# Sums by source: deeper rings, and SyncE reads its start places four at a time without a range check

## The chip, the cores and the metric

One core of one Trainium2 chip runs the whole program. The metric is the device time of one execution, in microseconds (us); lower is better.

## The reference

A graph of 6250 nodes (256 features each) and 100000 edges (sorted by target `dst`) goes through four graph layers. What matters here is what layers 0 and 1 sum over the edges of one node:

```python
h = relu(layernorm(x))
support = h @ weight                                  # layer 0
msgs = support[src_or_dst] * edge_weight[:, None]
out = segment_sum(msgs, ..., num_segments=6250)       # summed by the edge's source
edge_proj = edge_attr @ W_sum + b_sum                 # layer 1
sum3d = segment_sum(edge_proj, src, num_segments=n)   # by source too
out_deg = segment_sum(ones, src, num_segments=n)
```

In layer 0 the call passes `src` as the row to sum into and `dst` as the row to read. So for each source node three things are summed over its edges: the weighted rows h[dst] (256 numbers), the edge attributes (128 numbers), and a count (1). The products with the weights come after the sums. Layers 2 (attention by target) and 3 (a gated update with relation vectors) follow; the change does not touch them.

## The kernel before, in words

The program is a chain of stages with a barrier between them: `prepare` (ranks the edges by source and scatters one record per edge into DRAM), `source_sums`, `layers_0_and_1`, `attention`, `layer_2`, `relations_and_layer_3`. Five engines run their own instruction streams and meet at semaphores.

`source_sums` (L721 to L841) is the stage that the change touches. `src_records` holds the edges' records in order of source: 128 attributes, a one, the source, the target, the weight (132 floats, `REC`). Nodes lie in 49 blocks of 128. A tile is 128 consecutive records that belong to one block; there are `TILES` = 832 of them, whatever the graph, so the last ones of the list are empty: their start place is clamped to EDGES, where 128 padding records lie, all of them with target 0. About 100000/128 + 49/2, some 806 tiles, hold edges. One tile passes through these steps:

- SyncE (L755 to L761) has the tile's start place in a register and issues the load of its 128 records into `s_rec[k]`. Before it reuses a slot it waits until the tile that had the slot is summed (L760). A turn is `UNROLL` = 8 tiles. At its head (L756) SyncE reads eight start places into registers, and for each a range check runs: one FUSED_REGOPS and one SEQ_ASSERT.
- ScalarE (L773, L774) turns the target into an integer index and the source into a place within the block.
- GpSimd (L781, L782) waits for that index and issues an indirect DMA that gathers 128 rows of h, 1 KB each, into `s_row[k]`.
- VectorE (L811, L813) makes two one-hot matrices of 128x128, `s_hot` and the weighted `s_hotw`.
- TensorE (L790 to L795) waits for both one-hots, for the gathered rows, and for the PSUM bank (four of them) to be free, then does two matmuls into one bank: weighted rows, and attributes with the count.
- VectorE (L820) adds the bank to the block's sums in `nodes`. It does so `LAG` = 4 tiles behind the one-hots, so in its stream add(t-4) stands behind hots(t). At a turn's head (L826) it reads the blocks of eight tiles into registers.

GpSimd has no wait of its own for a free row slot; that order comes from the index, which waits for the record, which waits for the tile `R` = 8 before to be summed. So SyncE's wait at L760 bounds how far the whole chain runs ahead: eight tiles. Every loop runs over turns of R tiles, and the loop's body is unrolled R times on each engine.

Of the kernel before, what the change touches and what calls it, by code (L numbers as in the profile page):

```python
# [21 lines left out]
SP_E, PE_E, DVE_E, ACT_E = (mybir.EngineType.SP, mybir.EngineType.PE, mybir.EngineType.DVE,  # L22
                             mybir.EngineType.Activation)

P = 128
NODES, D = 6250, 256
EDGES, ED = 100000, 128
# [5 lines left out]
UNROLL = 8  # L33
# [3 lines left out]
TILES = -(-(-(-EDGES // P) + BLOCKS) // (2 * UNROLL)) * 2 * UNROLL  # L37
TURNS = TILES // UNROLL
# [6 lines left out]
ONE, SRC, DST, WGT = ED, ED + 1, ED + 2, ED + 3  # L45
NW = D + ED + 1
# [2 lines left out]
ROUNDS = [len(range(k, BLOCKS, TURN_BLOCKS)) for k in range(TURN_BLOCKS)]  # L49
RELS = 16  # L50
ORDER_RANGE = "the order holds each block, 0 to BLOCKS - 1, once"
BLOCK_RANGE = "a tile's block is a count of blocks (1 to BLOCKS) less one, whatever the graph"
DEG_MAX = 511
EPS = 1e-5
# [666 lines left out]
def source_sums(env):  # L721

    nc, c, sb, ps, sem = (env[k] for k in ("nc", "c", "sb", "ps", "sem"))
    acc = env["nodes"]
    R = UNROLL
    LAG = 4
    with nc.cleanup_on_exit(), ExitStack() as ctx:
        rec = sb(ctx, "s_rec", [P, R, REC])
        row = sb(ctx, "s_row", [P, R, D])
        idx = sb(ctx, "s_idx", [P, R], I32)  # L730
        loc = sb(ctx, "s_loc", [P, R])
        hot = sb(ctx, "s_hot", [P, R, P])
        hotw = sb(ctx, "s_hotw", [P, R, P])
        blk = sb(ctx, "s_blk", [1, TILES], I32)
        start = sb(ctx, "s_start", [1, TILES], I32)
        blk_all = sb(ctx, "s_blk_all", [P, TILES], I32)
        nbase = sb(ctx, "s_nbase", [P, TILES])
        sums = [ps(ctx, f"s_sums{k}", [P, 512]) for k in range(4)]

        tables, cleared = sem("s_tables"), sem("s_cleared")  # L740
        rec_in = [sem(f"s_rec_in{k}") for k in range(R)]
        row_in = [sem(f"s_row_in{k}") for k in range(R)]
        idx_ready, loc_ready, hot_ready = sem("s_idx_ready"), sem("s_loc_ready"), sem("s_hot_ready")
        summed, added = sem("s_summed"), sem("s_added")

        with nc.Block() as block:
            @block.sync
            def _(sp):
                sp.dma_start(blk[:], env["table_rows"]["sb"][0:TILES, :].rearrange("t o -> o t")).then_inc(tables, 16)
                sp.dma_start(start[:], env["table_rows"]["ss"][0:TILES, :].rearrange("t o -> o t")).then_inc(tables, 16)  # L750
                sp.dma_start(blk_all[:], env["table_rows"]["sb"][0:TILES, :].rearrange("t o -> o t")
                             .broadcast_to([P, TILES])).then_inc(tables, 16)
                sp.wait_ge(tables, 48)

                def turn(g, opening):  # L755
                    _, firsts = nc.values_load_multi_w_load_instructions(  # L756
                        start[0:1, bass.ds(g * R, R)], engines=(SP_E,), min_val=0, max_val=EDGES)
                    for k in range(R):
                        if not opening:
                            sp.wait_ge(summed, g * R + (k - R + 1))  # L760
                        sp.dma_start(rec[:, k, :], env["src_records"][bass.ds(firsts[k], P), :]).then_inc(rec_in[k], 16)  # L761

                turn(0, True)
                with sp.Fori(1, TURNS) as g:
                    turn(g, False)

            @block.scalar
            def _(ac):
                ac.wait_ge(cleared, 2)
                with ac.Fori(0, TURNS) as g:  # L770
                    for k in range(R):
                        ac.wait_ge(rec_in[k], g * 16 + 16)
                        nc.scalar.activation(idx[:, k:k + 1], rec[:, k, DST:DST + 1], ACT.Copy).then_inc(idx_ready, 1)  # L773
                        nc.scalar.activation(loc[:, k:k + 1], rec[:, k, SRC:SRC + 1], ACT.Identity,  # L774
                                             bias=nbase[:, bass.ds(g * R + k, 1)]).then_inc(loc_ready, 1)

            @block.gpsimd
            def _(gp):
                with gp.Fori(0, TURNS) as g:
                    for k in range(R):  # L780
                        own_wait(gp, idx_ready, g * R + k + 1)  # L781
                        gp.indirect_dma_start(out=row[:, k, :], out_offset=None, in_=env["h0_rows"],  # L782
                                              in_offset=bass.IndirectOffsetOnAxis(ap=idx[:, k:k + 1], axis=0)
                                              ).then_inc(row_in[k], 16)

            @block.tensor
            def _(pe):
                def turn(g, opening):
                    for k in range(R):
                        pe.wait_ge(hot_ready, g * (2 * R) + 2 * k + 2)  # L790
                        pe.wait_ge(row_in[k], g * 16 + 16)
                        if not opening or k >= 4:
                            pe.wait_ge(added, g * R + (k - 4 + 1))
                        nc.tensor.matmul(sums[k % 4][:, 0:D], hotw[:, k, :], row[:, k, :], start=True, stop=True)  # L794
                        nc.tensor.matmul(sums[k % 4][:, D:NW], hot[:, k, :], rec[:, k, 0:ED + 1],  # L795
                                         start=True, stop=True).then_inc(summed, 1)

                turn(0, True)
                with pe.Fori(1, TURNS) as g:
                    turn(g, False)  # L800

            @block.vector
            def _(ve):
                nc.vector.memset(acc[:], 0.0).then_inc(cleared, 1)
                ve.wait_ge(tables, 48)
                nc.vector.tensor_scalar(nbase[:], blk_all[:], -float(P), None, ALU.mult).then_inc(cleared, 1)
                ve.wait_ge(cleared, 2)

                def hots(g, k):
                    ve.wait_ge(loc_ready, g * R + k + 1)  # L810
                    nc.vector.tensor_scalar(hot[:, k, :], c["iota"][:], loc[:, k:k + 1], None,  # L811
                                            ALU.is_equal).then_inc(hot_ready, 1)
                    nc.vector.tensor_scalar(hotw[:, k, :], c["iota"][:], loc[:, k:k + 1], rec[:, k, WGT:WGT + 1],  # L813
                                            ALU.is_equal, ALU.mult).then_inc(hot_ready, 1)

                def add(t, k, b):
                    ve.wait_ge(summed, t + 1)
                    ve.wait_ge(added, t)
                    s = acc[:, bass.ds(b, 1), :]
                    nc.vector.tensor_tensor(s, s, sums[k % 4][:, 0:NW].rearrange("p (a b) -> p a b", a=1),  # L820
                                            ALU.add).then_inc(added, 1)

                def turn(g, opening):
                    lo = 0 if opening else g * R - LAG
                    n = R - LAG if opening else R
                    _, blocks = nc.values_load_multi_w_load_instructions(  # L826
                        blk[0:1, bass.ds(lo, n)], engines=(DVE_E,), min_val=0, max_val=BLOCKS - 1,
                            skip_runtime_bounds_check_because=BLOCK_RANGE)
                    for k in range(R):
                        hots(g, k)  # L830
                        if not opening or k >= LAG:
                            add(g * R + (k - LAG), (k - LAG) % R, blocks[k - LAG if opening else k])

                turn(0, True)
                with ve.Fori(1, TURNS) as g:
                    turn(g, False)
                _, blocks = nc.values_load_multi_w_load_instructions(
                    blk[0:1, TILES - LAG:TILES], engines=(DVE_E,), min_val=0, max_val=BLOCKS - 1,
                            skip_runtime_bounds_check_because=BLOCK_RANGE)
                for k in range(LAG):  # L840
                    add(TILES - LAG + k, R - LAG + k, blocks[k])  # L841
# [962 lines left out]
def relations_and_layer_3(env):  # L1804
# [10 lines left out]
    with nc.cleanup_on_exit(), ExitStack() as ctx:  # L1815
# [35 lines left out]
        def ranked(q, engine):  # L1851

            _, (b,) = nc.values_load_multi_w_load_instructions(
                c["dord"][0:1, bass.ds(q, 1)], engines=(engine,), min_val=0, max_val=BLOCKS - 1,
                skip_runtime_bounds_check_because=ORDER_RANGE)
            return b
# [281 lines left out]
```

## Time and profile before

| what | value |
| --- | --- |
| runs | 5604.88, 5611.56, 5610.76 us; median 5610.76 |
| the profiled execution | 5615.93 us, of which the span (first to last instruction) 5614.1 us |
| `source_sums` | from about 1476 to 2572 us of the span: 1096 us |
| busy there | GpSimd 794.5, VectorE 851.3, TensorE 767.4, ScalarE 330.1 us |
| granted TensorE clock | 0.955 over the span, 0.98 in the stage |

"Busy" counts an engine's work, not its waits and not its sequencer's register and DMA-issuing instructions; SyncE has only such instructions and so no busy time. "Idle before" an instruction is the time in which its engine did nothing, and the arrow names what ended it: another engine's instruction, the landing of a DMA, or "issue", when nothing outside was waited for. The last piece of `source_sums` is the add of tile 831; the barrier and the cleanup behind it take about 2 us, and the next stage's loads follow.

### The profile page before, as it was taken

The page shows a single profiled execution, that of the slowest core. Times are in us where ns is not written, and L with a number is a line of the kernel's source. Part 1 is how long each engine was busy: PE and PEld are TensorE (multiplying, and loading weights), DVE is VectorE, ACT ScalarE, POOL GpSimd, SP SyncE. Part 2 cuts the span into 40 slices and gives each one's busy share as a digit, 9 for nine tenths or more (in the row PEclk, how much of TensorE's full clock was granted, in tenths as well). Part 3 has the DMA queues.
Part 4 walks back from the last instruction along what each step waited for, and adds up shares of the span by engine and source line. Part 5 has one row for each costly group of instructions (what it writes and reads, how often), then busy time and mean ns, then how long its engine had stood idle before and what let it go on. Part 6 is the DMA issues. An engine that isn't in the chain of part 4 may idle for free. (4 is left out here: it accounts for less than half of the span.)

```text
span 5614.1 us, 108115 instructions
## 1 busy us (share of the span) xinstructions
PE 3530.3 (63%) x16558; PEld 2634.7 (47%) x16559; DVE 3950.7 (70%) x14077; ACT 1757.7 (31%) x6303; POOL 3898.1 (69%) x4332
## 2 busy tenths in 40 slices
PE   0000035200277777776768999999989778888887
PEld 0000012100255555554547888888879644554444
DVE  9918999300477777774568888888868766666665
ACT  0000000000133333332337777777756411111111
POOL 2878887776477777775766666666647777676774
PEclk9999999999999999997879999999999889899998
DMA  2232233335355555554323333333322233333332
GB/s 75 76 84 79 76 82 88 87 88 125 76 156 157 157 158 155 157 157 93 94 86 96 94 94 94 95 94 95 94 66 66 88 111 114 103 110 106 108 108 78
DMA packets 491102, 578.41 MB, mean 103 GB/s; under 512 B 114758, under 2 KB 394328, under 8 KB 490945
## 3 DMA queue, kind: packets, MB, share of 16 engines
q0 software_dynamic: 189536, 397.34, 25.4%
q1 hardware_dynamic: 301473, 180.10, 11.8%
q14 instruction: 67, 0.55, 0.0%
q8 instruction: 26, 0.43, 0.0%
HBM read 491.28 MB, written 86.57 MB: 103 GB/s over the span
## 5 line engine op out<-in xcount | busy, mean ns | idle before, releaser
L410 POOL DMA_INDIRECT src_records<-rec,pos_slot x800 | 1005.0, 1256 | 345.2 <-issue 237.0
L1289 POOL DMA_INDIRECT a_row<-h_rows,a_idx x832 | 787.6, 947 | 369.8 <-PE a_p_s L1415 197.1
L1905 POOL DMA_INDIRECT r_row<-h_rows,r_idx x832 | 802.1, 964 | 310.2 <-issue 168.2
L782 POOL DMA_INDIRECT s_row<-h_rows,s_idx x832 | 794.5, 955 | 299.7 <-issue 171.7
L794 PE MATMUL s_sums<-s_row,s_hotw 128*128 128x256 f32 x1664 | 584.9, 434 | 329.8 <-DMA s_row<-h_rows,s_idx 231.7
L1946 PE MATMUL r_p_s<-r_row,r_hot 128*128 128x272 f32 x1664 | 602.2, 474 | 233.2 <-DVE r_row L2080 215.1
L1392 PE MATMUL a_p_q<-nodes,a_hotT 128*128 x1664 | 569.8, 424 | 55.5 <-DVE a_score L1459 54.1
L1946 PEld LDWEIGHTS r_p_s<-r_row,r_hot 128*128 128x128 f32 x1664 | 335.4, 221 | 516.8 <-DVE r_row L2080 233.8
L820 DVE TENSOR_TENSOR nodes<-nodes,s_sums 128x385 f32 x832 | 461.5, 555 | 157.1 <-PE s_sums L795 138.7
L1415 PE MATMUL a_p_s<-a_row,a_masked 128*128 128x257 f32 x1664 | 497.0, 380 | 2.1 <-DVE sums L1496 1.4
L794 PEld LDWEIGHTS s_sums<-s_row,s_hotw 128*128 128x128 f32 x1664 | 253.0, 192 | 477.1 <-issue 369.6
L2088 DVE TENSOR_TENSOR sums<-sums,r_p_s 128x272 f32 x832 | 358.6, 431 | 149.3 <-PE r_p_s L1946 103.2
L773 ACT ACTIVATE s_idx<-s_rec 128x1 int32<-128x1 f32 x832 | 167.9, 202 | 863.3 <-DMA s_rec<-src_records 731.3
L1496 DVE SCALAR_TENSOR_TENSOR sums<-sums,a_fade,a_p_s 128x257 f32 x832 | 399.3, 480 | 41.7 <-PE a_p_s L1415 3.7
L1459 DVE CUSTOM_DVE_ANT_0 a_prod<-a_p_q,a_row 128x258 f32<-128x258 f32 x832 | 353.5, 425 | 104.9 <-ACT a_masked L1338 63.3
L795 PEld LDWEIGHTS s_sums<-s_rec,s_hot 128*128 128x128 f32 x1664 | 323.0, 194 | 46.1
L477 ACT ACTIVATE pos_slot<-pos_src 125x8 int32 x100 | 20.9, 209 | 1014.8 <-DMA rec<-in_edge_attr 991.4
L1415 PEld LDWEIGHTS a_p_s<-a_row,a_masked 128*128 128x128 f32 x1664 | 314.5, 190 | 49.5 <-ACT a_masked L1359 2.3
L795 PE MATMUL s_sums<-s_rec,s_hot 128*128 128x129 f32 x1664 | 326.2, 278 | 0.0
L1338 ACT ACTIVATE a_masked<-a_far,a_score 128x128 f32<-128x128 f32 x832 | 323.7, 389 | 2.0 <-DVE a_score L1459 2.0
L1359 ACT ACTIVATE a_masked<-a_masked,a_mneg 128x128 f32<-128x128 f32 x832 | 324.2, 390 | 0.0
L504 PE MATMUL p_total<-cnt,ones 125*128 125x49 f32 x4 | 1.3, 432 | 492.2 <-DVEq L559 492.2
(308 smaller groups left out, 8747.5 us busy)
## 6 DMA issues: line engine op xcount, KB each, us to landing
s_rec<-src_records SPq DMA_DIRECT2D x832, 66.0 KB
rec<-in_edge_attr SPq DMA_DIRECT2D x100, 500.0 KB
s_row<-h_rows,s_idx POOLq DMA_INDIRECT x832
a_row<-h_rows,a_idx POOLq DMA_INDIRECT x832, 2.8
r_row<-h_rows,r_idx POOLq DMA_INDIRECT x832, 2.8
src_records<-rec,pos_slot POOLq DMA_INDIRECT x800
h_rows<-H SPq DMA_DIRECT2D x1, 6272.0 KB
x_rows<-nodes SPq DMA_DIRECT2D x49, 128.0 KB, 1.9
```

What stands on the lines that cost most here:

```text
L410: gp.indirect_dma_start(out=src_records, out_offset=bass.IndirectOffsetOnAxis(ap=pos_slot[:, k:k + 1], axis=0), in_=rec[:, k, :], in_offse ...
L782: gp.indirect_dma_start(out=row[:, k, :], out_offset=None, in_=env["h0_rows"], in_offset=bass.IndirectOffsetOnAxis(ap=idx[:, k:k + 1], axis=0)
L794: nc.tensor.matmul(sums[k % 4][:, 0:D], hotw[:, k, :], row[:, k, :], start=True, stop=True)
L795: nc.tensor.matmul(sums[k % 4][:, D:NW], hot[:, k, :], rec[:, k, 0:ED + 1], start=True, stop=True).then_inc(summed, 1)
L820: nc.vector.tensor_tensor(s, s, sums[k % 4][:, 0:NW].rearrange("p (a b) -> p a b", a=1), ALU.add).then_inc(added, 1)
L1289: gp.indirect_dma_start(out=row[:, k, 0:D], out_offset=None, in_=env["h2_rows"], in_offset=bass.IndirectOffsetOnAxis(ap=idx[:, k:k + 1], a ...
L1392: nc.tensor.matmul(p_q[k % 2], hotT[:, k % F, :], query[:, bass.ds(b, 1), 0:RW].rearrange("p a d -> p (a d)"), start=True, stop=True).then ...
L1415: nc.tensor.matmul(p_s[k % 2], masked[:, k % F, :], row[:, k, 0:D + 1], start=True, stop=True).then_inc(S["summed"], 1)
L1496: nc.vector.scalar_tensor_tensor(out=s, in0=s, scalar=fade[:, k % F:k % F + 1], in1=p_s[k % 2], op0=ALU.mult, op1=ALU.add).then_inc(S["add ...
L1905: gp.indirect_dma_start(out=row[:, k % R, 0:D], out_offset=None, in_=env["h3_rows"], in_offset=bass.IndirectOffsetOnAxis(ap=idx[:, k:k + 1 ...
L1946: nc.tensor.matmul(p_s[k % 4], hot[:, k % H, :], row[:, k % R, :], start=True, stop=True).then_inc(S["summed"], 1)
L2088: nc.vector.tensor_tensor(s, s, p_s[k % 4], ALU.add).then_inc(S["added"], 1)
```

## The change

In `source_sums` alone:

- `R`, the number of slots of the rings `s_rec`, `s_row`, `s_idx`, `s_loc` and of the semaphores `s_rec_in`, `s_row_in`, goes from 8 to 16. The one-hot rings stay at `H` = 8. SyncE may now be sixteen tiles ahead of the sums.
- As R is also the unroll, each loop has 52 turns of 16 tiles in place of 104 of 8, on all engines. VectorE reads sixteen blocks at a turn's head in place of eight.
- SyncE reads its start places four at a time, ahead of tiles 0, 4, 8 and 12 of a turn, and the range check is left out.

The short description of the change also names "the attention in spread steps"; the diff holds no line of the attention, which is the same before and after.

```diff
+START_RANGE = "a start is the lesser of EDGES and a sum of counts, whatever the graph"
...
-    R = UNROLL
+    R = 2 * UNROLL
+    H = UNROLL
     LAG = 4
+    turns = TILES // R
...
-        hot = sb(ctx, "s_hot", [P, R, P])
-        hotw = sb(ctx, "s_hotw", [P, R, P])
+        hot = sb(ctx, "s_hot", [P, H, P])
+        hotw = sb(ctx, "s_hotw", [P, H, P])
...
                 def turn(g, opening):
-                    _, firsts = nc.values_load_multi_w_load_instructions(
-                        start[0:1, bass.ds(g * R, R)], engines=(SP_E,), min_val=0, max_val=EDGES)
                     for k in range(R):
+                        if k % 4 == 0:
+                            _, firsts = nc.values_load_multi_w_load_instructions(
+                                start[0:1, bass.ds(g * R + k, 4)], engines=(SP_E,), min_val=0, max_val=EDGES,
+                                skip_runtime_bounds_check_because=START_RANGE)
                         if not opening:
                             sp.wait_ge(summed, g * R + (k - R + 1))
-                        sp.dma_start(rec[:, k, :], env["src_records"][bass.ds(firsts[k], P), :]).then_inc(rec_in[k], 16)
+                        sp.dma_start(rec[:, k, :], env["src_records"][bass.ds(firsts[k % 4], P), :]).then_inc(rec_in[k], 16)
 
                 turn(0, True)
-                with sp.Fori(1, TURNS) as g:
+                with sp.Fori(1, turns) as g:
                     turn(g, False)
...
-                        nc.tensor.matmul(sums[k % 4][:, 0:D], hotw[:, k, :], row[:, k, :], start=True, stop=True)
-                        nc.tensor.matmul(sums[k % 4][:, D:NW], hot[:, k, :], rec[:, k, 0:ED + 1],
+                        nc.tensor.matmul(sums[k % 4][:, 0:D], hotw[:, k % H, :], row[:, k, :], start=True, stop=True)
+                        nc.tensor.matmul(sums[k % 4][:, D:NW], hot[:, k % H, :], rec[:, k, 0:ED + 1],
                                          start=True, stop=True).then_inc(summed, 1)
```

The loops of ScalarE, GpSimd, TensorE and VectorE run over `turns` in place of `TURNS`, and VectorE writes the one-hots at `k % H`.

## Rows read from the trace of the kernel before

**Rows 1.** The page: costliest groups; count, busy us, mean ns, idle before, releaser.
```profile
L782 POOL DMA_INDIRECT s_row<-h_rows,s_idx x832 | 794.5, 955 | 299.7 <-issue 171.7
```
**Rows 2.** Busy by engine in one window: PE, PEld, DVE, ACT, POOL, clock, DMA share.
```profile
1476.00:2572.00 1096.00, 767.35 (x3328) 574.12 (x3328) 851.32 (x2498) 330.13 (x1664) 794.48 (x832) 0.98 0.56 151
```
**Rows 3.** Waits from 1498 to 2516: us in total, times, longest us.
```profile
ACT s_idx L773 <- DMA s_rec<-src_records: 695.8, 718, 6.8
...
POOL s_row L782 <- issue: 166.8, 546, 0.6
...
POOL s_row L782 <- ACT s_idx L773: 83.3, 258, 2.0
```
**Rows 4.** Timeline of POOL: start us, us, idle before; the seven longest gaps before 2516.
```profile
1641.06 0.94 POOL L782 DMA_INDIRECT s_row<-h_rows,s_idx  x1 [1.85 <-ACT s_idx L773]
...
1775.04 0.95 POOL L782 DMA_INDIRECT s_row<-h_rows,s_idx  x1 [0.80 <-ACT s_idx L773]
...
1909.07 0.94 POOL L782 DMA_INDIRECT s_row<-h_rows,s_idx  x1 [0.46 <-issue]
...
2042.87 0.94 POOL L782 DMA_INDIRECT s_row<-h_rows,s_idx  x1 [0.61 <-issue]
...
2165.42 0.94 POOL L782 DMA_INDIRECT s_row<-h_rows,s_idx  x1 [0.75 <-ACT s_idx L773]
...
2178.46 0.94 POOL L782 DMA_INDIRECT s_row<-h_rows,s_idx  x1 [1.99 <-ACT s_idx L773]
...
2312.80 0.94 POOL L782 DMA_INDIRECT s_row<-h_rows,s_idx  x1 [0.80 <-ACT s_idx L773]
```
**Rows 5.** Waits from 2516 to 2571.
```profile
POOL s_row L782 <- ACT s_idx L773: 16.5, 11, 5.8
```
**Rows 6.** Gather packets, MB, share, in 2490:2510, 2525:2535, 2535:2540, 2555:2560, in this order.
```profile
q0 software_dynamic: 766, 2.09, 33.9%
...
q0 software_dynamic: 259, 0.69, 77.1%
...
q0 software_dynamic: 81, 0.21, 23.4%
...
q0 software_dynamic: 118, 0.33, 34.5%
```
**Rows 7.** Timeline of the stage's end: the last gather, the last add.
```profile
2562.01 0.94 POOL L782 DMA_INDIRECT s_row<-h_rows,s_idx  x1 [0.30 <-issue]
...
2569.51 0.56 DVE L820 TENSOR_TENSOR nodes<-nodes,s_sums 128x385 f32 x1 [0.58 <-PE s_sums L795]
```
**Rows 8.** SyncE by source line (ns min/median/max), and its own waits from 1530 to 2516.
```profile
L756 SPq FUSED_REGOPS  x832: 147/147/188, 1480.4 to 2541.9; - x167
...
L756 SPq TENSOR_LOAD <-s_start x104: 521/525/743, 1479.6 to 2539.6; - x104
...
L761 SPq DMA_DIRECT2D s_rec<-src_records x832: 332/333/366, 1482.6 to 2556.6; - x167
...
SPq L761 <- PE s_sums L795: 246.6, 341, 1.2
```
**Rows 9.** VectorE's register loads by source line: 4, 8 and 16 blocks at once.
```profile
L837 DVEq TENSOR_LOAD <-s_blk x1: 352/352/352, 2562.3 to 2562.3; - x1
...
L826 DVEq TENSOR_LOAD <-s_blk x104: 594/599/610, 1495.9 to 2548.4; - x104
...
L1440 DVEq TENSOR_LOAD <-dblk x53: 1348/1351/1368, 2965.8 to 4115.8; - x53
```
**Rows 10.** Instruction queues from 1480 to 1530, and TensorE's timeline there.
```profile
q8 instruction: 1, 0.02, 0.1%
q14 instruction: 2, 0.02, 0.1%
...
1514.35 1.22 PE L794 MATMUL s_sums<-s_row,s_hotw 128*128 128x256 f32 x2 [2.12 <-DMA s_row<-h_rows,s_idx]
```

More of the change, by code:

```diff
@@ L769, in _ @@
                 ac.wait_ge(cleared, 2)
-                with ac.Fori(0, TURNS) as g:
+                with ac.Fori(0, turns) as g:
                     for k in range(R):
@@ L778, in _ @@
             def _(gp):
-                with gp.Fori(0, TURNS) as g:
+                with gp.Fori(0, turns) as g:
                     for k in range(R):
@@ L793, in turn @@
                             pe.wait_ge(added, g * R + (k - 4 + 1))
-                        nc.tensor.matmul(sums[k % 4][:, 0:D], hotw[:, k, :], row[:, k, :], start=True, stop=True)
-                        nc.tensor.matmul(sums[k % 4][:, D:NW], hot[:, k, :], rec[:, k, 0:ED + 1],
+                        nc.tensor.matmul(sums[k % 4][:, 0:D], hotw[:, k % H, :], row[:, k, :], start=True, stop=True)
+                        nc.tensor.matmul(sums[k % 4][:, D:NW], hot[:, k % H, :], rec[:, k, 0:ED + 1],
                                          start=True, stop=True).then_inc(summed, 1)
                 turn(0, True)
-                with pe.Fori(1, TURNS) as g:
+                with pe.Fori(1, turns) as g:
                     turn(g, False)
@@ L810, in hots @@
                     ve.wait_ge(loc_ready, g * R + k + 1)
-                    nc.vector.tensor_scalar(hot[:, k, :], c["iota"][:], loc[:, k:k + 1], None,
+                    nc.vector.tensor_scalar(hot[:, k % H, :], c["iota"][:], loc[:, k:k + 1], None,
                                             ALU.is_equal).then_inc(hot_ready, 1)
-                    nc.vector.tensor_scalar(hotw[:, k, :], c["iota"][:], loc[:, k:k + 1], rec[:, k, WGT:WGT + 1],
+                    nc.vector.tensor_scalar(hotw[:, k % H, :], c["iota"][:], loc[:, k:k + 1], rec[:, k, WGT:WGT + 1],
                                             ALU.is_equal, ALU.mult).then_inc(hot_ready, 1)
@@ L834, in _ @@
                 turn(0, True)
-                with ve.Fori(1, TURNS) as g:
+                with ve.Fori(1, turns) as g:
                     turn(g, False)
```

## The prediction

> **What bounds the stage now.** I read the page first: among its four costliest groups is GpSimd's row gather of this stage, 832 instructions of 955 ns, with 299.7 us of idle before them, most of it "issue" [rows 1]. Then the busy times of the stage's window. Per tile of 832 they are VectorE 851.3/832 = 1.02 us (with the one clearing of `nodes` in it), GpSimd 0.955, TensorE 0.92, ScalarE 0.40 [rows 2]. No engine is full at 1096/832 = 1.32 us per tile, so the next question is what the gaps are made of.
>
> The waits answer it. From 1498 to 2516 GpSimd sat idle 166.8 us for "issue" in 546 gaps, 0.305 us each, and 83.3 us with ScalarE's index as the last event in 258 gaps, 0.323 us each [rows 3]. The two means are nearly the same. The 0.30 us is the floor between two indirect DMAs and stands before every one of them, whoever is named. So the index is named as releaser but costs next to nothing: GpSimd's own step, 0.945 + 0.305 = 1.25 us, is the pace. ScalarE's 695.8 us of waiting for the record's landing [rows 3] is the sum that catches the eye, and it is the wrong one: ScalarE is 0.40 us of work in a 1.25 us step and is idle anyway.
>
> Where the record does decide can be counted. In the timeline only seven gaps before 2516 are clearly over the floor, 1.85, 0.80, 0.46, 0.61, 0.75, 1.99 and 0.80 us, 7.26 together; less 7 x 0.30 that is 5.2 us [rows 4]. Behind 2516, in the empty tiles at the end of the list, ScalarE's index ends 11 gaps of 16.5 us; less 11 x 0.30 that is 13.2 us [rows 5]. All that a deeper ring can take from GpSimd is therefore 5.2 + 13.2 = 18.4 us, 0.3% of the time.
>
> **The ring of 16, full tiles.** A record load is now issued when the tile sixteen before is summed. At 1.25 us per tile that is 8 x 1.25 = 10 us more notice. The longest of the seven late records cost 1.7 us over the floor, so all seven go: -5.2 us. What is late next is nothing but GpSimd's own step, which the change leaves as it is. Bounds: 0 (if what delays the record delays GpSimd's step as well) to 5.2. I take 5.2.
>
> **The ring of 16, empty tiles.** Here the sum of waits is not the gain. All records of an empty tile name target 0, and the gathers get slow. A tile has 766/16 = 48 packets at normal pace, 16 gathers in 20 us. In the stretch 2525:2535 259 packets went through in 10 us with the queue at 77% of the 16 DMA engines: 26 packets per us, 1.85 us per tile, slower than GpSimd's 1.25 [rows 6]. So the end is set by the transfers: 26 empty tiles need 26 x 1.85 = 48 us however early they are issued. The ring gives back only the time in which the gathers ran dry behind GpSimd's stalls: in 2535:2540 81 packets went in place of 130, in 2555:2560 118 [rows 6], 61 packets or 2.3 us. I take -2 us. The bounds are 0 and the whole 13.2. The row gather of the last tile starts 7.5 us ahead of the last add now [rows 7]; I expect that distance to grow to some 18 us, as GpSimd gets ahead of transfers that don't speed up.
>
> **SyncE's four reads and no check.** Per turn of 8 there were 8 checks of 147 ns and one register read of 525 ns [rows 8]. A read of four took VectorE 352 ns, of eight 599 [rows 9], so I put SyncE's read of four at 0.35 us, between 0.26 (half of 0.525) and 0.525. Before: 832 x 0.147 + 104 x 0.525 = 177 us. After: 208 x 0.35 = 73 us. SyncE is rid of about 100 us of 1096. It is worth 0 on the path: it waited 246.6 us for the sums within 986 us [rows 8], so it is not full. The head of a turn does make the first records of each turn late, but that is inside what GpSimd's floor already hides, and where it isn't hidden it is in the 5.2 and 13.2 us counted above. With the range check still there, the deeper ring would give the same.
>
> **VectorE's read of sixteen blocks.** 1.351 us once in 16 tiles, for 2 x 0.599 = 1.198 [rows 9]: 52 x 0.153 = 8 us more in VectorE's stream. VectorE needs 1.02 us of 1.25 per tile, 0.23 x 16 = 3.7 us of slack a turn, against one pause of 1.35. I take 0; if all of it came through, +8.
>
> **The rest.** Sixteen more semaphores to clear and 16 loads ahead of the first wait in place of 8: SyncE's eight more loads in the opening, some 0.6 us each, fall into VectorE's clearing of `nodes`. The one-hot ring of 8 is not felt: add(t-5) stands ahead of hots(t) in VectorE's stream. 0 within half a microsecond.
>
> **Sum.** 5.2 + 2 = 7 us less. The profiled execution took 5615.93 us and would take 5609; it lies 5.2 us above the median of the runs, 5610.76, so the forecast for the median is 5610.8 - 7 = 5604 us.
>
> **Rivals.**
> *Nothing comes of it.* The end of the stage is set by transfers, and what is won before 2516 could be taken back if the disturbances that made records late slow the row gathers too. Then 5611, same. For it: the seven gaps come at a regular distance (about 134 us between several of them [rows 4]), as something of the DMA side would. Against: GpSimd's pace beside them is unchanged.
> *The tail is not bound by transfers.* If the slow packets are slow because record loads and gathers collide in bursts, an even flow could run at GpSimd's 1.25 us per tile. Then all 18.4 us come: 5592, faster. Against: the stretch 2525:2535 was full at 77% with the gathers alone [rows 6].
> *The doubled bodies stop fitting.* The slower side. Every engine's loop body is now 16 tiles long. In the first turns, 1480 to 1530, three instruction packets were moved, and TensorE stood 2.12 us for a late gather beside them [rows 10]. From 1530 to 2580 no instruction packet is in the view: an 8-tile body is fetched once and stays. If GpSimd's body of 16 had to be fetched anew each turn, at such a 2.12 us, that were 51 x 2.12 = 108 us: 5712. It decides from (11.2 + 7)/51 = 0.36 us a turn. Against: the attention's loops are unrolled 32 times on every engine, and between 3030 and 4090 no instruction packet is in the view either. On the other engines a pause of 2 us in 16 x 0.23 = 3.7 us of slack would be hidden.
> The Trainium skill ("Runtime: NRT & Kernel Launch", "Instruction fetch mechanics") states this rule: a taken branch whose target lies outside the engine's two resident pages stalls until the page is fetched. If the doubled body fell outside them the sum would be 5712 by the rule, and 5604 if it stays inside; the attention's loops, without a fetch, speak for the second.
>
> **How the numbers follow.** A measurement of this kernel can tell about 0.2%, 11.2 us, from no change. Chances: forecast (gain of 3 to 11) 0.50; nothing (0 to 3, or VectorE's +8) 0.22; the tail's full gain 0.20; bodies, or another loss over 11 us, 0.08. "Faster" is the full gain's 0.20 and 0.03 of the forecast's, "slower" 0.08, "same" the rest, 0.69. The range goes from 5592 (all 18.4) to 5614 (nothing gained, and half of VectorE's 8 us lost).
>
> **What would show it.** GpSimd's gaps before the gather: no more than two over 0.35 us before the empty tiles, and "idle before" down from 299.7 to about 281. ScalarE's wait for records stays large or grows in count, and means nothing. SyncE's checks gone, its wait for the sums up by about 100 us or more. The last gather issued near 2544, the last add near 2563. If the last add comes near 2552 the tail was not bound by transfers; if any GpSimd gap stands at each turn of 16, or instruction packets appear between 1530 and 2560, the third rival has it. The forecast is wrong if the stage's length changes by more than 12 us or if time moves in another stage.

## The result, and the profile after

The changed kernel is slower: 5675.63 us median (5669.95 to 5680.53, four runs) against 5611.16 (5604.88 to 5616.32, four runs), a ratio of 1.0115 [1.0098, 1.0133], some 64.5 us. The profiled execution took 5680.53 us with a span of 5678.7, 64.6 more than the span before. The forecast was 5604 and a range up to 5614.

The first question is where the time is. Each stage ends with an instruction that clears the semaphores, so its length can be read off (us):

| kernel | prepare | source_sums | layers 0/1 | attention | layer 2 | relations |
| --- | --- | --- | --- | --- | --- | --- |
| before | 1475.3 | 1096.6 | 365.2 | 1185.1 | 326.6 | 1165.0 |
| after | 1472.6 | 1081.3 | 364.6 | 1260.9 | 327.6 | 1171.5 |

The stage that was changed gained 15.3 us, twice the forecast. The attention, of which the diff holds no line, lost 75.8, and the relations stage, which is not touched either, 6.5.

The two stages of after, busy by engine (columns as in [rows 2]):

```profile
1473.00:2554.00 1081.00, 770.63 (x3328) 572.99 (x3328) 843.12 (x2498) 335.54 (x1664) 789.04 (x832) 0.98 0.58 153
2922.00:4179.00 1257.00, 1149.46 (x6656) 993.28 (x6656) 990.76 (x3749) 893.14 (x3121) 788.26 (x832) 0.96 0.30 88
```

And the attention of before:

```profile
2941.00:4122.00 1181.00, 1106.34 (x6656) 965.34 (x6656) 995.56 (x3749) 884.56 (x3119) 787.57 (x832) 0.99 0.32 93
```

The attention does the same work: as many instructions, and VectorE even 5 us less busy. (TensorE's busy time grew with a granted clock of 0.96 for 0.99.) So time went into gaps. The waits of the attention after (engine, tile and line, what came last; us, times, longest):

```profile
POOL a_row L1294 <- PE a_p_s L1420: 171.9, 280, 5.2
...
DVE a_prod L1464 <- issue: 107.3, 28, 4.5
POOL a_row L1294 <- ACT a_idx L1310: 101.6, 26, 6.0
```

and before:

```profile
POOL a_row L1289 <- PE a_p_s L1415: 197.1, 322, 2.1
...
POOL a_row L1289 <- ACT a_idx L1305: 7.3, 4, 3.9
...
DVE a_prod L1459 <- issue: 6.0, 5, 4.3
```

VectorE stood still 28 times for up to 4.5 us with "issue" as the reason: by the profile no other engine and no data made it wait. Its loop passes its branch 25 times and turns back at 24 of them. One place in VectorE's timeline of after, at a turn's head:

```profile
3058.78 0.47 DVE L1501 SCALAR_TENSOR_TENSOR sums<-sums,a_fade,a_p_s 128x257 f32 x1
3063.30 0.43 DVE L1464 CUSTOM_DVE_ANT_0 a_prod<-a_p_q,a_row 128x258 f32<-128x258 f32 x1 [4.05 <-issue]
```

Around them lie the loop's branch at 3058.65, the next record of VectorE's sequencer at 3061.47, and the register load of 1.37 us. Over the 25 passes the median from the end of VectorE's branch to the next sequencer record is 0.23 us before and 2.85 us after; ScalarE's goes from 0.17 to 0.19 us and GpSimd's from 0.11 to 0.21. The queues point at the cause. From the page of after (packets, MB, share):

```profile
q14 instruction: 188, 1.54, 0.1%
q8 instruction: 27, 0.44, 0.0%
```

from the page of before:

```profile
q14 instruction: 67, 0.55, 0.0%
```

and from the view of the DMA between 3030 and 4090, where before has no such row, after has

```profile
q14 instruction: 111, 0.91, 0.3%
```

These are 121 packets more of 8192 bytes, five for each turn behind a taken branch. So VectorE fetches its attention loop anew in every turn. The loop has 317 instructions. Two packets come right behind the branch, and the others when VectorE has passed some 44, 172 and 296 instructions of the loop, about 128 apart. So code comes in pieces of 128 instructions, and 8192/128 makes 64 bytes for one. The change made VectorE's code of `source_sums` longer, from 104 instructions to 192: 88 more stand ahead of the attention. The places of the packets fit a loop that began at a piece's start and lay in three pieces (317 of 384), and that now begins 88 behind one (88 + 317 = 405) and lies in four. The experiments test this.

The Trainium skill ("Runtime: NRT & Kernel Launch", "Instruction fetch mechanics") says that instruction memory is, for most engines, 32 KiB or 512 instructions, in two lines of 16 KiB, and that a taken branch to a page outside the resident ones stalls for a fetch. The trace agrees on the stall and on 64 bytes for an instruction. It differs on the size of a fetch: VectorE's packets are 8 KiB. And a loop of 317 instructions, well under 512, is fetched anew. The four pieces that it touches are together 4 x 128 = 512 instructions, and a turn moves five. That a piece is read ahead and puts the loop's first one out would fit both numbers; no run here shows it.

The changed stage itself, first GpSimd's timeline at its end (the last gathers):

```profile
2536.41 0.95 POOL L787 DMA_INDIRECT s_row<-h_rows,s_idx  x1 [2.82 <-ACT s_idx L778]
2540.28 0.95 POOL L787 DMA_INDIRECT s_row<-h_rows,s_idx  x1 [2.92 <-ACT s_idx L778]
2546.05 0.94 POOL L787 DMA_INDIRECT s_row<-h_rows,s_idx  x1 [4.83 <-ACT s_idx L778]
2547.30 0.94 POOL L787 DMA_INDIRECT s_row<-h_rows,s_idx  x1 [0.30 <-issue]
```

VectorE's last add:

```profile
2552.71 0.56 DVE L825 TENSOR_TENSOR nodes<-nodes,s_sums 128x385 f32 x1 [0.21 <-DVE nodes L825]
```

SyncE's read of four places (ns min/median/max), the landing of its record loads, and its wait for the sums:

```profile
L761 SPq TENSOR_LOAD <-s_start x208: 294/298/508, 1476.7 to 2520.3; - x104
```

```profile
DMA to landing us min/median/max: 1.7/1.9/19.4
```

```profile
SPq L766 <- PE s_sums L800: 422.4, 686, 1.8
```

and the gather's group on the page, against [rows 1]:

```profile
L787 POOL DMA_INDIRECT s_row<-h_rows,s_idx x832 | 789.0, 948 | 293.1 <-ACT s_idx L778 210.0
```

### The profile page after: what moved, and what is told of

Read it like the earlier page. It is cut to its first block and busy times, and to the rows that moved or that the text cites. A ratio compares the mean times of both kernels' runs of the same rounds, so it can differ in the third digit from the quotient of the medians.

```text
span 5678.7 us, 105999 instructions
## 1 busy us (share of the span) xinstructions
PE 3588.6 (63%) x16558; PEld 2669.3 (47%) x16559; DVE 3931.3 (69%) x14077; ACT 1770.9 (31%) x6303; POOL 3898.0 (69%) x4332
## 5 line engine op out<-in xcount | busy, mean ns | idle before, releaser
L787 POOL DMA_INDIRECT s_row<-h_rows,s_idx x832 | 789.0, 948 | 293.1 <-ACT s_idx L778 210.0
L1951 PE MATMUL r_p_s<-r_row,r_hot 128*128 128x272 f32 x1664 | 616.1, 483 | 228.6 <-DVE r_row L2085 220.6
L1397 PE MATMUL a_p_q<-nodes,a_hotT 128*128 x1664 | 588.3, 436 | 86.3 <-DVE a_score L1464 54.8
L1420 PE MATMUL a_p_s<-a_row,a_masked 128*128 128x257 f32 x1664 | 509.7, 388 | 3.6 <-DVE sums L1501 2.9
```

Of the source, the lines that this page charges most:

```text
L1397: nc.tensor.matmul(p_q[k % 2], hotT[:, k % F, :], query[:, bass.ds(b, 1), 0:RW].rearrange("p a d -> p (a d)"), start=True, stop=True).then ...
L1420: nc.tensor.matmul(p_s[k % 2], masked[:, k % F, :], row[:, k, 0:D + 1], start=True, stop=True).then_inc(S["summed"], 1)
L1951: nc.tensor.matmul(p_s[k % 4], hot[:, k % H, :], row[:, k % R, :], start=True, stop=True).then_inc(S["summed"], 1)
```

## The experiments

Two theories for the attention. *Place:* only where the loop stands against the pieces of 128 matters. *Something else of the change:* the registers held by a body of 16 tiles, the rings' semaphores, the state in which the stage leaves the chip. The instrument is instructions without work in VectorE's stream of `source_sums`, run once, ahead of its loop:

```diff
                 nc.vector.memset(acc[:], 0.0).then_inc(cleared, 1)
+                for _ in range(N):
+                    ve.nop(nofuse=True).then_inc(spare, 1)
```

They shift all of VectorE's code behind them and cost next to nothing where they stand (`source_sums` with 128 of them takes 1093.5 us, without them 1096.6). All stage lengths first (us), with the loop's start within a piece as counted from the kernel before, start + 317 against the 384 of three pieces, and the median from the end of VectorE's branch to the next sequencer record in the attention:

| kernel | start, end | source_sums | attention | relations | VectorE's branch |
| --- | --- | --- | --- | --- | --- |
| before | 0, 317 | 1096.6 | 1185.1 | 1165.0 | 0.23 |
| after | 88, 405 | 1081.3 | 1260.9 | 1171.5 | 2.85 |
| e1 after + 64 | 24, 341 | 1085.1 | 1184.7 | 1177.8 | 0.25 |
| e2 before + 88 | 88, 405 | 1096.7 | 1260.9 | 1175.3 | 2.87 |
| e3 SyncE's part alone | 0, 317 | 1088.7 | 1185.0 | 1166.2 | 0.23 |
| e4 e1 with the check | 24, 341 | 1084.9 | 1184.8 | 1178.2 | 0.25 |
| e5 after + 40 | 0, 317 | 1084.9 | 1185.2 | 1173.5 | 0.25 |
| e6 before + 60 | 60, 377 | 1097.9 | 1185.1 | 1175.6 | 0.21 |
| e7 before + 72 | 72, 389 | 1098.7 | 1270.3 | 1178.6 | 3.19 |
| e8 e5, targets spread | 0, 317 | 1069.6 | 1185.6 | 1174.7 | 0.25 |
| e9 e3, targets spread | 0, 317 | 1075.7 | 1185.8 | 1163.7 | 0.23 |
| e10 before + 128 | 0, 317 | 1093.5 | 1185.3 | 1171.9 | 0.25 |
| e11 before, relations + 40 | 0, 317 | 1094.2 | 1185.0 | 1169.8 | 0.23 |

Each row is one profiled execution. Equal code differs between them by some us: `prepare`, which eleven of the thirteen kernels share, takes 1469 to 1475 us, and `source_sums` 1096.6 in before and 1094.2 in e11. The attentions without the stall agree within 1.1 us. The ratios below are of whole times, against the kernel before as it ran beside each group: medians 5609.85 us for e1 to e4, 5618.7 for e5 to e8, 5619.33 for e9 to e11.

**e1, the change with N = 64.**

> The changed kernel with 64 more instructions on VectorE alone (each adds one to a semaphore that nobody waits for), put behind the clearing of nodes in source_sums; what is computed is unchanged. Theory A (place of VectorE's code): in the changed kernel VectorE's attention loop, 317 instructions, stands 88 instructions further back than before, so that it reaches over one more of the 128-instruction pieces in which the trace shows code being loaded, and is loaded anew each turn; VectorE stands 2.8 us at each of 25 loop branches. 64 instructions move it on to another place (24 behind a piece's start by my count), the 2.8 us go and the attention returns from 1261 to 1185 us: 5675.6 - 76 = 5600 us, and the extra instruction packets between 3030 and 4150 are gone. Theory B (the deeper ring itself, its semaphores or its memory, slows the attention): no change, 5676 us or a few us more.

5608.44 us against 5609.85, 0.9997 [0.9988, 1.0006]. The attention's loss is gone, 1184.7:

```profile
DVE a_prod L1466 <- issue: 6.1, 5, 4.3
```

From 3030 to 4090 no instruction packet is left. All of the change is in this kernel, so nothing else that it does in its own stage slows the attention. 5600 us were expected; the 8 us that are missing lie mostly in the relations stage (1177.8 for 1171.5 in after) and in `source_sums` (1085.1 for 1081.3).

**e2, the kernel before with N = 88.**

> The kernel before with the same kind of instruction, 88 of them, at the same place on VectorE. Nothing of the change is in it. Theory A: VectorE's attention loop then stands exactly where it stands in the changed kernel, so the attention takes 76 us more and source_sums is as before: 5611 + 76 = 5687 us, with instruction packets at each turn of the attention. Theory B: 5611 us, up to 5 more for the instructions themselves.

5684.87 us, 1.0131 [1.0116, 1.0147]: the loss without any of the change, 1260.9 to the tenth. Its waits in the attention and its instruction packets from 3030 to 4090:

```profile
DVE a_prod L1461 <- issue: 106.9, 28, 4.4
POOL a_row L1291 <- ACT a_idx L1307: 106.0, 27, 6.0
```

```profile
q14 instruction: 113, 0.93, 0.3%
```

**e6 and e7, the kernel before with N = 60 and 72,** on the two sides of the limit of 384.

> The kernel before with 60 more instructions on VectorE. By my count the attention loop then starts 60 behind a piece's start and ends at 60 + 317 = 377, within three pieces of 128 = 384. Theory A says no reload: attention 1185 us, the whole 5611 us and up to 10 more from the relations' stage. Rival A' (any place but the old one reloads, or the limit is another one, such as half of this): 5687 us.

> The same with 72 instructions: 72 + 317 = 389 is past 384, into a fourth piece. Theory A: attention 1261 us, the whole 5687 us, and instruction packets at each turn of the attention. If it comes out as the one with 60, four pieces are not the limit and theory A has the right loop and the wrong count.

e6: 5622.09 us, 1.0007 [0.9998, 1.0016]; e7: 5716.39 us, 1.0177 [1.0162, 1.0193]. Twelve instructions without work are the whole difference and cost 85 us in the attention. That is 9 us more than the 1261 expected: behind the branch VectorE stands 3.19 us in e7 for 2.85 in after. Why it is longer there was not tested. e6's row and e7's:

```profile
DVE a_prod L1461 <- issue: 6.4, 5, 4.3
```

```profile
DVE a_prod L1461 <- issue: 116.4, 28, 4.9
```

and e7's instruction packets from 3030 to 4090:

```profile
q14 instruction: 112, 0.92, 0.3%
```

Inside the loop e7's packets come after some 55, 188 and 316 instructions. The loop starts 16 instructions earlier in its piece than in after, and the packets come 11 to 20 later in the loop: they stay with the places in the code. The limit lies where three pieces end, and it tells the loop's start in the kernel before to between 4 instructions ahead of a boundary and 7 behind it.

**e10, N = 128,** a whole piece.

> The kernel before with 128 instructions without work in VectorE's stream of source_sums, so that everything behind stands exactly 128 instructions later, at the same place within its piece. Theory of pieces of 128: attention touches three pieces, 1185 us, no wait behind the branch (0.23 us). A rival, that the shift as such or the number of added instructions makes the loop reload: 1260 us or more. For the longer relations stage: if it is the place of VectorE's code within the pieces, 1165 us here and 5613 in all; if any added instruction in an earlier stage does it, 1175 us and 5622.

5617.74 us, 1.0001 [0.9992, 1.0011]. The largest shift of all leaves the attention at 1185.3. It is the place within a piece, not the amount of added instructions.

**e3, SyncE's part alone, rings of eight.**

```diff
-                    _, firsts = nc.values_load_multi_w_load_instructions(
-                        start[0:1, bass.ds(g * R, R)], engines=(SP_E,), min_val=0, max_val=EDGES)
                     for k in range(R):
+                        if k % 4 == 0:
+                            _, firsts = nc.values_load_multi_w_load_instructions(
+                                start[0:1, bass.ds(g * R + k, 4)], engines=(SP_E,), min_val=0, max_val=EDGES,
+                                skip_runtime_bounds_check_because=START_RANGE)
```

> The kernel before with SyncE's part of the change alone: start places read in fours, no range check, rings 8 deep. Theory (SyncE is not on the path): 5611 us within 4, the stage's length within 4 us of 1097; its seven gaps of GpSimd before the empty tiles still there. Rival (the head of a turn on SyncE is what makes records late): most of the 15 us that the stage won come already here, 5598 us. Theory A says of both that the attention is as before, 1185 us, as VectorE's code has not moved.

5604.37 us, 0.9989 [0.998, 0.9998]; the stage 7.9 us shorter, and all seven gaps of [rows 4] gone with rings of eight. The expectation that SyncE is not on the path fails; of the rival's 15 us about half came. **e4, e1 with the range check kept:**

```diff
-                                skip_runtime_bounds_check_because=START_RANGE)
+                                )
```

> The changed kernel with the 64 instructions on VectorE, and SyncE's range check back in (reads still in fours, rings 16 deep). Theory (the ring gives the stage's gain, the check costs nothing): as the kernel with 64 instructions and no check, 5600 us within 4, stage 1081 us. Rival (the check is part of it): 8 us or more above that one.

5611.33 us, 1.0002 [0.9993, 1.0011], the stage 1084.9 as in e1. Beside the deeper ring the check costs nothing. So SyncE's part without the deeper ring brings 7.9 us, and the whole change, its attention mended (e1, e5), 11.5 to 11.7. The ring with reads of eight was not run, nor reads of four with the check on rings of eight: what the ring is worth alone, and which half of SyncE's part took the gaps away, stays open.

**e5, the change with N = 40,** which puts the loop where it was, one whole piece further on.

> The changed kernel with 40 more instructions on VectorE in place of 64. 88 + 40 = 128, one whole piece, so every loop of VectorE behind source_sums stands against the pieces as in the kernel before. The kernel with 64 came out at 5608 and not at the 5600 that I expected; its source_sums had its 12 us, its attention was as before, and the relations' stage took 1178 us in place of 1165, at a lower granted clock. Theory C (the place of VectorE's code sets the relations' stage too, through something other than a reload): here it is 1165 us again and the whole 5597 us. Theory D (the relations' stage is slowed by what else the change moved: the code of the other engines, the ring): 5608 us as with 64, relations near 1178 us.

5610.88 us, 0.9987 [0.9978, 0.9996]. The attention is back, the relations stage is not (1173.5).

**e8, e5 with the padding records' targets 0 to 127 in place of 0.** These records hold zeros, and the add of an empty tile does not change with them.

```diff
+                nc.gpsimd.tensor_copy(tail[:, DST:DST + 1], pidx_i[:]).then_inc(iotas, 1)
                 nc.gpsimd.memset(tail[:, SRC:SRC + 1], -1.0).then_inc(tail_ready, 1)
...
-                gp.wait_ge(iotas, 7)
+                gp.wait_ge(iotas, 8)
```

> The changed kernel with 40 instructions on VectorE, and the padding records behind the last edge name targets 0 to 127 in place of 128 times target 0 (their source stays -1, so they add nothing, and the output is the reference's). Theory (the slow gathers of the 26 empty tiles come from 128 reads of one row): they run at GpSimd's 1.25 us per tile, from the first empty tile's gather to the last add some 25 x 1.25 + 5 = 36 us in place of 49: 13 us less than the kernel with 40 instructions alone, 5584 us if that is at 5597. Rival (record loads and gathers collide, or TensorE's clock holds the tail): within 4 us of it.

5595.79 us, 0.9959 [0.9945, 0.9972]. From the gather of tile 806 to the last add it takes 36.0 us for e5's 51.5. The gather queue from 2515 to 2545 in after, then from 2510 to 2535 in e8:

```profile
q0 software_dynamic: 853, 2.32, 77.5%
```

```profile
q0 software_dynamic: 960, 2.62, 36.7%
```

28 packets per us at 77.5% of the engines' time against 38 at 36.7%. With 48 packets per tile that is 1.69 and 1.25 us; the second is GpSimd's own step. 128 reads of one row are what makes the gather slow, not the number of reads. The stage is 15.3 us shorter than e5's, 13 were expected.

**e9, SyncE's part and the spread targets,** rings of eight, no VectorE code moved.

> The kernel before with SyncE's reads in fours without the range check (rings stay at 8, no VectorE instruction is moved), and with the padding records' targets set to 0..127 in place of 0 for all. The results do not change, as the padding records are summed into no block's rows that are read. If the two gains add: source_sums 1088.7 (SyncE alone) less the tail's 15 us = about 1074 us, relations 1166 as with SyncE alone, attention 1185; 5590 us, ratio 0.9965. If a ring of eight holds the tail back although the gathers are quick (each record load waits for the tile eight before): source_sums 1080 or more, 5597. If the relations stage becomes longer as in the run that spread the targets with moved VectorE code: 1175, 5600.

5594.79 us against 5619.33, 0.9960 [0.9946, 0.9974]. The gains add: `source_sums` 1075.7 (1074 expected), relations 1163.7. The end of the stage on GpSimd:

```profile
2535.76 0.95 POOL L786 DMA_INDIRECT s_row<-h_rows,s_idx  x1 [0.30 <-issue]
2537.01 0.94 POOL L786 DMA_INDIRECT s_row<-h_rows,s_idx  x1 [0.30 <-issue]
```

Even the last gathers stand at the floor of 0.30 us with rings of eight. e8 and e9 are faster than the kernel before by 0.4%; between them the intervals do not decide.

**e11, 40 instructions without work at the head of the relations stage alone.**

> The kernel before with 40 instructions without work at the head of VectorE's stream of the relations stage alone, behind the clearing of its sums; all stages ahead of it are the kernel's before, instruction for instruction. If the place of VectorE's relations code is what makes this stage longer: 1173 to 1179 us. If it is what ran before it (the added instructions or the changed source_sums, through the granted clock): 1165 us, and the mean low-clock time of the stage near 271 us.

5617.03 us, 0.9998 [0.9989, 1.0008]; the stage 1169.8. It lies between the two expectations and does not decide between them.

**What the relations stage shows.** In the three kernels in which VectorE's code is the kernel's before (before, e3, e9) it takes 1163.7 to 1166.2 us, in the ten others 1169.8 to 1178.6. Its branches show no stall (0.22 to 0.23 us from a branch's end to the next record), and e10, with each instruction at the same place within its piece, has 1171.9, so the pieces do not seem to explain it. What goes with the length is the granted clock: of this stage 263 to 279 us stand at the lower level in those three kernels, 298 to 376 in the others, and the longest stages have the most of it. The windows of before and of e1 show it in TensorE's busy time, for as many matmuls:

```profile
4450.00:5613.00 1163.00, 929.66 (x2923) 554.22 (x2923) 767.76 (x2841) 133.56 (x456) 802.13 (x832) 0.88 0.37 106
```

```profile
4440.00:5612.00 1172.00, 960.81 (x2923) 581.25 (x2923) 769.53 (x2841) 133.44 (x456) 806.47 (x830) 0.85 0.36 105
```

The clock doesn't fall more often, it stays low longer: 49 to 51 stretches at the lower level in every one of the thirteen kernels. Why, and whether it is the cause or follows from small stalls of VectorE, stays open. A stall behind a branch is excluded. The difference is 5 to 14 us of 5610, in one execution each, and for e10 and e11 the whole time shows no loss (1.0001 [0.9992, 1.0011] and 0.9998 [0.9989, 1.0008]). For e1 it shows one: `source_sums` gave 11.5 us and the whole time less than 2.

## Why the prediction was wrong

- **The step that failed** is in the rival of the bodies that stop fitting (0.08 with any other loss), in its "against": "the attention's loops are unrolled 32 times on every engine, and between 3030 and 4090 no instruction packet is in the view either". The row was right and the inference was not. That a loop isn't fetched anew says that it fits where it stands, not that it fits wherever it is put. VectorE's attention loop had 384 - 317 = 67 instructions of reserve, and the change moved it by 88 (e2, e6, e7, e10). I looked for the risk in the body that grew and not in the unchanged loop behind it, and on GpSimd, where the slack was small, and not on VectorE. The last sign that the prediction names, time moving in another stage, is what came.
- **Its price** was right for the wrong place: 2.12 us a turn was expected from one early stall [rows 10]; measured were 2.85 - 0.23 = 2.6 us behind the branch, and 75.8/25 = 3.0 us a turn of the stage, at 24 branches in place of 51. That the two prices are near each other is luck.
- **What hid the stall** was wrong too. "On the other engines a pause of 2 us in 16 x 0.23 = 3.7 us of slack would be hidden": that slack is a mean, and of `source_sums`. In the attention VectorE's "issue" waits grew from 6 to 107 us and came through as 76 us of stage; GpSimd's wait for ScalarE's index, for one, grew from 7.3 to 101.6 us. Part of the 76 us may be the clock: the attention has 24 us at the lower level before, 99 in after and e2, and 106 in e7. It goes with the stall in all of them; its share was not measured.
- **Full tiles:** the seven gaps went, 5.2 us, as forecast, though e3 shows that they go without the ring too. Not forecast: the gathers became shorter, 955 to 948 ns. From the first gather to that of tile 806 it is 1020.7 us before and 1009.9 after, 10.8 less: 5.3 of idle time and 5.5 of instructions. Of these 806 gathers 144 take over 0.97 us before; it is 114 to 144 in the kernels that keep SyncE's code and the rings of eight, some 81 to 94 in e3, e4 and e9, and 32 to 43 in the kernels with the whole of it (after, e1, e5, e8). What makes a gather long was not tested.
- **Empty tiles:** forecast -2, measured 52.3 to 49.1 us, -3.2. That they are bound by transfers is shown by e8, and the rival that they are not fails. The distance from the last gather to the last add was to grow to 18 us and shrank from 7.5 to 5.4. The reason is in the timeline above: GpSimd ran dry again, 2.82, 2.92, 4.83 us, behind records that landed late (up to 19.4 us, median 1.9), beside the slow gathers; with the targets spread the longest landing is 2.8 us (e9), with rings of eight and slow gathers 6.6 (e3). So GpSimd's idle time went from 299.7 to 293.1 us, not to 281. The prediction had "if the last add comes near 2552" as a sign against the transfers; it came there, 2552.71, because the stage began 2.7 us earlier and the front gave 10.8. A sign of that kind must be a distance, not a time.
- **SyncE was worth 0:** wrong by itself. e3 takes 7.9 us off the stage. A wait of 246.6 us for the sums showed that SyncE is not full on average; the head of a turn, with eight checks and a read of eight, was nevertheless what made the seven records late, since with its part alone they aren't. The sentence that the deeper ring would give the same with the check holds (e4, with reads of four).
- **VectorE's read of sixteen** was not tested alone; the stage got shorter with it, so no loss of 8 us stands out. SyncE's read of four took 0.298 us, forecast 0.35.

Sum by stage, after less before: -2.7 in prepare, -15.3 in `source_sums` (forecast -7; -11.5 to -11.7 in e1 and e5, whose stage does the same work), -0.6, +75.8, +1.0, and +6.5 in the relations stage; 64.7 us, the span's 64.6.

## What to carry to other kernels

When an edit changes the number of instructions on an engine, every later loop of that engine moves against the pieces in which code is fetched. Count the pieces that each long loop touches before and after (on VectorE here 128 instructions each), and look in the profile for instruction packets in the steady state and for "issue" gaps once per turn. A few instructions without work, run once, put the loop back: here 40 of them took 75.7 us from the attention (1260.9 to 1185.2). And padding that points to one address can be slower than real work: spread it.

## What the runs showed of the hardware

- The queue that brings VectorE's attention loop, q14, moves 8192 bytes a packet (before: 67 packets, 0.55 MB), the other, q8, 16 KB (after: 27, 0.44 MB). Whether q14 serves other engines too was not looked at. VectorE's loop of 317 instructions, the one loop measured, is kept when it touches three pieces of 128; when it touches four it is fetched anew each turn, at 2.6 us behind the branch or more (e7: 3.19 - 0.23 = 3.0).
- 128 reads of one DRAM row by an indirect DMA come at 26 to 28 packets per us, spread over 128 rows at 38, where GpSimd's own step sets the pace. Beside the slow ones record loads landed up to 19.4 us after issue (after), beside the spread ones up to 2.8 (e9).
- In the slow tail of after the granted clock is 0.50, the lower level, while TensorE works 22.8 of 30 us; in e9's tail it is 1.00:

```profile
2515.00:2545.00 30.00, 22.79 (x57) 16.68 (x58) 14.96 (x45) 2.84 (x14) 14.34 (x16) 0.50 0.86 95
```

```profile
2510.00:2540.00 30.00, 21.84 (x97) 16.19 (x97) 22.65 (x67) 7.72 (x38) 21.25 (x23) 1.00 0.50 143
```

After has 57 matmuls in it and e9 97, in nearly the same busy time. Even at the lower level TensorE is not full there.

- A register load takes 0.30 us for four registers on SyncE, 0.525 for eight [rows 8], and 1.35 for sixteen on VectorE [rows 9].
